# Rewriting the order of every engine as a table of slots: each step its own slot, three batches and 32 weight tiles placed one by one, then a repeating pattern; four feed-forward banks; most low halves of the weights taken by VectorE

## What is computed

```python
x = x + xattn(_layernorm(x), ctx, ctx, q_norm_w, k_norm_w, w_out)   # 16 heads, 4 key/value heads, causal
x = x + ffn(_layernorm(x), ...)
# xattn: q, k = rope(rms_norm(.) * w); attn = softmax(q k^T / sqrt(32) + causal mask); out = (attn v) @ w_out.T
# ffn, once for all batches: w = (w_q - 7.5) * scale per 64 columns, transposed     (4-bit codes, 512 x 2048 and 2048 x 512)
y1 = x1 @ w_up + b_up + x1 @ lora_a @ lora_b
x2 = relu(y1)
y2 = x2 @ w_down + b_down + x2 @ lora_a' @ lora_b'
```

## Time and profile before

| | |
|---|---|
| median of 3 runs | 587.93 us (584.47 to 588.89) |
| the profiled execution's own time | 587.63 us |
| its span, first to last instruction | 585.8 us |
| mean granted clock of TensorE | 0.929 of full speed (2.4 GHz) |
| first UP of batch 0 starts | 130.69 us into the span |
| result of batch 0 and of batch 15 written by DVE from | 171.8 us and 582.6 us |
| PE busy from the one to the other | 388.80 of 410.80 us |

### The profile page before, as it was taken

The page is one execution under the profiler, slowest core; times in us unless marked ns, Lnnn a source line. Parts: engine busy times, 40 slices in busy tenths (PEclk is TensorE's granted clock), DMA queues, the critical chain, the costliest instruction groups (busy, mean ns, idle before and its releaser), DMA issues.

```text
span 585.8 us, 12700 instructions
## 1 busy us (share of the span) xinstructions
PE 490.9 (84%) x4744; PEld 343.0 (59%) x4744; DVE 342.3 (58%) x1042; ACT 315.9 (54%) x947; POOL 301.4 (51%) x320
## 2 busy tenths in 40 slices
PE   0267456679888999989999989899999898999997
PEld 0134122337547676667677676767585757586783
DVE  2873513344456777675767758576767676564531
ACT  1557636373565665747484837383847464654210
POOL 3492474483174838383847556556657473625100
PEclk9999555759999999998999999899999998999999
DMA  8930652081053527180817282735455444536010
GB/s 171 284 84 2 191 131 62 29 190 32 10 89 88 123 56 139 39 167 10 167 21 157 39 138 47 131 61 118 56 122 98 84 95 57 103 52 109 2 38 18
DMA packets 144253, 52.87 MB, mean 90 GB/s; under 512 B 132768, under 2 KB 135088, under 8 KB 144144
## 3 DMA queue, kind: packets, MB, share of 16 engines
q1 hardware_dynamic: 141344, 51.56, 43.3%
q10 hardware_dynamic: 2768, 0.34, 0.5%
q0 software_dynamic: 80, 0.16, 0.1%
HBM read 16.39 MB, written 4.19 MB: 35 GB/s over the span
## 4 chain that ended last, share of the span: by engine, by line
PE 45%; POOL 20%; DMA 10%; issue 8%; ACT 6%; DVE 6%; SPq 5%; POOLq 0%; ACTq 0%; DVEq 0%
PE ff L767 19%; PE ff L782 8%; DMA pT<-big 8%; PE tb L748 8%; POOL big L396 6%; POOL pr L387 5%; PE ff L638 3%; SPq L326 3%; POOL y L436 3%; PE tb L735 2%; ACT pr L543 2%; PE sb L720 1%; PE ff L683 1%; POOL inv L379 1%; DVE x L978 1%
## 5 line engine op out<-in xcount | busy, mean ns | idle before, releaser
L767 PE MATMUL ff<-xnT,wu_hi 128*128 128x128 f16 x2048 | 184.2, 223 | 2.7 <-DVE y L1045 1.2
L767 PE MATMUL ff<-xnT,wu_lo 128*128 128x128 f16 x1024 | 180.4, 223 | 0.0
L767 PEld LDWEIGHTS ff<-xnT,wu_hi 128*128 128x128 f16 x2048 | 162.3, 100 | 13.7 <-issue 7.4
L782 PE MATMUL ff<-wd_hi,x 128*128 128x512 f16 x512 | 152.4, 379 | 3.1 <-DVE z L930 2.3
L387 POOL TENSOR_TENSOR pr<-pr,rinv 128x512 f32<-128x512 f32 x64 | 74.5, 1164 | 137.3 <-DVE rinv L911 137.3
L605 ACT ACTIVATE x<-z 128x512 f16<-128x512 f32 x64 | 40.3, 630 | 119.5 <-DVE z L930 119.5
L767 PEld LDWEIGHTS ff<-xnT,wu_lo 128*128 128x128 f16 x1024 | 102.4, 100 | 0.0
L543 ACT ACTIVATE pr<-pr,nmax 128x128 f32<-128x128 f32 x256 | 98.7, 388 | 4.3 <-DVE nmax L999 4.3
L782 PE MATMUL ff<-wd_lo,x 128*128 128x512 f16 x256 | 97.0, 379 | 0.0
L782 PEld LDWEIGHTS ff<-wd_hi,x 128*128 128x128 f16 x512 | 48.8, 98 | 63.4 <-issue 4.9
L396 POOL TENSOR_TENSOR big<-pr,big 128x512 f16<-128x512 f32 x64 | 78.7, 1238 | 3.4 <-ACT big L574 3.4
(11 more groups left out here) (139 smaller groups left out, 716.0 us busy)
## 6 DMA issues: line engine op xcount, KB each, us to landing
xt<-in_x SPq DMA_DIRECT2D x16, 256.0 KB, 3.1
big<-in_L_ffn_w_up_q SPq DMA_DIRECT2D x4, 1024.0 KB, 11.8
big<-in_L_ffn_w_down_q SPq DMA_DIRECT2D x4, 1024.0 KB, 5.4
out<-y SPq DMA_DIRECT2D x16, 256.0 KB, 2.5
kvt<-in_ctx SPq DMA_DIRECT2D x16, 64.0 KB, 3.3
wd_lo<-in_L_xattn_w_out SPq DMA_DIRECT2D x1, 1024.0 KB, 14.1
pT<-big SPq DMA_TRANSPOSE x64, 3.4
wd_hi<-in_L_ffn_w_up_lora_b SPq DMA_DIRECT2D x3, 128.0 KB, 8.6
```

Of the source, the lines that this page charges most:

```text
L767: last = pe.matmul(bank[:, P * h:P * h + P], a[:, m, cols], b[:, m, :], start=(h == 0 and m == 0 and i == 0), stop=(m == KC - 1 and i == 2 ...
L782: last = pe.matmul(ff[down_bank[n]][:], a[:, h, :], b[:, h, :], start=(h == 0 and i == 0), stop=(h == HC - 1 and i == 2))
```

## The change

The tables are replaced. Each operation of each engine now has its own table (`R_PHIGH`, `R_PLOW` and `R_PTURN` where `R_PSPLIT` served three engines), with four numbers: slots of batches 0, 1, 2 and 3; batch n from 3 on comes 264 slots after batch n-1. Each of the 32 tiles has a slot of its own for dequantising, turning, high half, rest and low half, and so have the five late loads, the lora pieces and the steps of w_out. Beside the order:

- the feed-forward has four banks (`ff0` to `ff3`); the bank of v's sum (`vb`) is given up, the sum goes into `tb[0]`, which PROJ also uses, and each waits for the other's reader;
- 22 of the 32 low halves are taken by DVE straight from bank minus high half (`weights_low`), without PE's subtraction; ten stay as they were;
- 17 tiles are dequantised by DVE (16 before), 15 by POOL; w_out is reordered by DVE instead of ACT; the scales of w_up are loaded from ACT's queue;
- the first tile waits for one lora copy (`a_copied`) instead of three.

The lora product opens a tile's bank and four turns add to it, as before.

```diff
-PERIOD = 8
-R_STATS, R_CENTRE, R_SINES, R_COSINES, R_ROPE = (0, 1), (1, 2), (1, 3), (1, 4), (2, 6)
-R_KSPLIT, R_KLOW = (1, 3), (1, 4)
-R_QSPLIT, R_QLOW = (2, 7), (2, 8)
...
+PERIOD, FREE = 264, 3
+R_STATS = (0, 369, 517, 922)
...
+R_PROBS = ((343, 737, 1108, 1389), (373, 745, 1135, 1417), (431, 785, 1216, 1541), (454, 787, 1255, 1592))
...
+R_POW2 = (606, 1090, 1504, 1785)
+R_YBASE = (714, 1169, 1638, 2002)
...
-TILE_AT = tuple(2 + (3 * t) // 4 if t < UP_TILES else 14 + (t - 16) // 2 if t < 26 else t - 7 for t in range(TILES))
-DEQ_LEAD = 4
-DVE_TILES = tuple(range(0, TILES, 2))
-WOUT_AT = 4
+DVE_TILES = (1, 2, 4, 6, 8, 10, 12, 14, 16, 18, 20, 22, 24, 26, 29, 30, 31)
+LOW_BY_DVE = (1, 3, 4, 6, 7, 10, 13, 15, 16, 17, 18, 19, 20, 22, 23, 24, 25, 26, 28, 29, 30, 31)
...
+TURN_AT = (206, 224, 233, 295, 443, 451, 458, 468, 487, 488, 508, 534, 583, 593, 595, 601, 649, 666, 744, 764, 806, 810, 892,
+           896, 907, 923, 951, 974, 980, 995, 1058, 1073)
...
+LOAD_AT = (141, 513, 580, 682, 741)
...
+WO_ORDER_AT = (259, 307, 353, 367)
...
-    SLOTS = PERIOD * (B - 2) + R_RESULT[1] + 1
-
-    def at(s, r, after=0):
-        if s - after == r[0]:
-            return 0
-        n, rest = divmod(s - after - r[1], PERIOD)
-        return n + 1 if rest == 0 and 0 <= n < B - 1 else None
+    SLOTS = PERIOD * (B - FREE - 1) + R_STORE[FREE] + 1
+
+    def at(s, r):
+        if s in r[0:FREE]:
+            return r.index(s)
+        n, rest = divmod(s - r[FREE], PERIOD)
+        return n + FREE if rest == 0 and 0 <= n < B - FREE else None
...
-        ff = [bank("ff0"), bank("ff1")]
+
+        ff = [bank("ff0"), bank("ff1"), bank("ff2"), bank("ff3")]
         sbk = [bank("sb0"), bank("sb1")]
 
         tb = [bank("tb0"), bank("tb1")]
-        vb = bank("vb")
 
...
+        def low_of(t):
+            return (w_low_v, LOW_BY_DVE.index(t) + 1) if t in LOW_BY_DVE else (w_low, t + 1 - len([u for u in LOW_BY_DVE if u < t]))
+
+        def wait_lows(eng, last):
+            by_dve = len([u for u in LOW_BY_DVE if u <= last])
+            if by_dve <= last:
+                eng.wait_ge(w_low, last + 1 - by_dve)
+            if by_dve:
+                eng.wait_ge(w_low_v, by_dve)
...
+        def next_bank():
+            b = (last_bank + 1) % 4
+            return (b + 1) % 4 if b == down_holds else b
...
+            for t in range(TILES):
+                if TURN_AT[t] == s:
+                    last_bank = t % 4 if t < UP_TILES else 2 + t % 2
+                    tile_bank[t], tile_free[t] = last_bank, freed_by[last_bank]
+                    freed_by[last_bank] = low_of(t)
...
-                n = at(s, R_KLOW)
+                n = at(s, R_KTURN)
...
-                    if TILE_AT[4 * (g - W_RING) + 3] == s:
+                    if LOAD_AT[g - W_RING] == s:
...
-                for t in tiles_to_dequantise(s):
-                    if t not in DVE_TILES:
+                for t in range(TILES):
+                    if DEQ_AT[t] == s and t not in DVE_TILES:
                         dequant(t)
-                n = at(s, R_STATS)
-                if n is not None:
+                n = at(s, R_KEYS)
+                if n:
                     keys(n)
+                n = at(s, R_POW)
+                if n is not None:
+                    norm_factors(n)
...
-            def order_wout():
-                act.wait_ge(wout_in, 16)
-                for j in range(KC):
-                    act.activation(wo_nat[:, j, :].rearrange("p (n g d) -> p n g d", g=NG, d=HD),
-                                   wo_raw[:, j, :].rearrange("p (g n d) -> p n g d", g=NG, d=HD),
-                                   ACT.Copy).then_inc(wo_ordered, 1)
-
...
+                for t in range(TILES):
+                    if HIGH_AT[t] == s:
+                        weights(t)
+                    if LOW_AT[t] == s and t not in LOW_BY_DVE:
+                        weights_low(t)
...
-                if t < 2:
-                    pe.wait_ge(a_copied, 3)
-                else:
+                if tile_free[t]:
                     pe.wait_ge(*tile_free[t])
                 g, j = divmod(t, 4)
-                if t in (0, UP_TILES // 4):
-                    pe.wait_ge(b_high, 1 if t == 0 else 3)
-                    pe.wait_ge(b_low, 1 if t == 0 else 3)
                 bank = ff[tile_bank[t]]
+                if t in (0, 4, UP_TILES):
+                    pe.wait_ge(a_copied, 3 if t == UP_TILES else 1)
+                    pe.wait_ge(b_high, 1 if t == 0 else 2 if t == 4 else 3)
+                    pe.wait_ge(b_low, 1 if t == 0 else 2 if t == 4 else 3)
                 if t < UP_TILES:
                     a, b = a_up3[:, P * j:P * j + P], b_up3[:, 512 * g:512 * g + 512]
...
-                    if n > 0:
+                    if n == 0:
+                        pe.wait_ge(wo_low, NN)
+                    else:
                         pe.wait_ge(v_arg_ready, n)
-                    pe.matmul(vb[:, 0:1], ones[:], ssq[:, n % 2:n % 2 + 1], start=True, stop=True).then_inc(v_summed, 1)
+                        if projs_before[n] > 0:
+                            pe.wait_ge(x1_ready, projs_before[n])
+                    pe.matmul(tb[0][:, 0:1], ones[:], ssq[:, n % 2:n % 2 + 1], start=True, stop=True).then_inc(v_summed, 1)
...
-                ts = tiles_at(s)
-                for i, t in enumerate(ts):
-                    weights(t)
-                    if i > 0:
-                        weights_rest(t - 1)
-                if WOUT_AT <= s < WOUT_AT + NN:
-                    wout_turn(s - WOUT_AT)
+                for i in range(3):
+                    if LORA_TURN_AT[i] == s:
+                        lora_turn(i)
+                for t in range(TILES):
+                    if REST_AT[t] == s and t not in LOW_BY_DVE:
+                        weights_rest(t)
+                    if TURN_AT[t] == s:
+                        weights(t)
+                for m in range(NN):
+                    if WO_TURN_AT[m] == s:
+                        wout_turn(m)
                 feed_forward(s)
-                for t in ts[-1:]:
-                    weights_rest(t)
                 products(s)
...
+            def wout_order(j):
+                if j == 0:
+                    dve.wait_ge(wout_in, 16)
+                dve.tensor_copy(wo_nat[:, j, :].rearrange("p (n g d) -> p n g d", g=NG, d=HD),
+                                wo_raw[:, j, :].rearrange("p (g n d) -> p n g d", g=NG, d=HD)).then_inc(wo_ordered, 1)
+
+            def weights_low(t):
+                dve.wait_ge(w_high, t + 1)
+                hi, lo = ((w[:, t % 4, 512 * (t // 4):512 * (t // 4) + 512] for w in (wu_hi, wu_lo)) if t < UP_TILES else
+                          (w[:, t - UP_TILES, :] for w in (wd_hi, wd_lo)))
+                dve.tensor_tensor(lo, ff[tile_bank[t]][:], hi, ALU.subtract).then_inc(w_low_v, 1)

```

More of the change, by code:

```diff
@@ L38 @@
-R_UP, R_DOWN = (18, 27), (22, 31)
-R_RESULT = (26, 35)
+PERIOD, FREE = 264, 3
+R_STATS = (0, 369, 517, 922)
+R_SQUARES = (2, 373, 523, 935)
+R_MOMENTS = (0, 441, 529, 968)
+R_KEYS = (0, 326, 621, 979)
+R_POW = (23, 496, 666, 994)
+R_CENTRE = (3, 464, 655, 1033)
+R_SINES = (2, 458, 720, 1019)
+R_COSINES = (28, 487, 676, 1083)
+R_ROPE = (218, 525, 754, 1063)
+R_KSPLIT = (7, 559, 747, 1040)
+R_KLOW = (176, 563, 837, 1076)
+R_KTURN = (19, 675, 897, 1074)
+R_QSPLIT = (172, 543, 779, 1097)
+R_QLOW = (231, 542, 835, 1120)
@@ new lines, in build @@
+        freed_by, last_bank, down_holds = [None] * 4, 3, None
+        def next_bank():
+            b = (last_bank + 1) % 4
+            return (b + 1) % 4 if b == down_holds else b
+        projs_before, sums_before = {}, {}
+        for s in range(SLOTS):
+            n = at(s, R_VSUM)
+            if n is not None:
+                projs_before[n] = len(sums_before)
+            n = at(s, R_PROJ)
+            if n is not None:
+                sums_before[n] = len(projs_before)
+        for s in range(SLOTS):
+            for t in range(TILES):
[3 more added lines that the diff above has]
+                    freed_by[last_bank] = low_of(t)
@@ L256, in build @@
+                n = at(s, R_DOWN[g])
+                if n is not None and g == 0:
+                    last_bank = down_holds = 0 if n == 0 else next_bank()
+                    down_bank[n], down_free[n] = last_bank, freed_by[last_bank]
+                    freed_by[last_bank] = (down_read, n + 1)
+                if n is not None and g == 3:
+                    down_holds = None
         block = es.enter_context(nc.Block())
@@ L1031, in values @@
             def values(s):
[L1032 removed]
+                n = at(s, R_VARG)
                 if n is not None:
```

315 lines of the change are left out of this document (168 added, 147 removed).

## The result

The changed kernel takes **531.89 us** (median of 4 runs, 529.08 to 532.98) against 587.44 us for the kernel before beside it (4 runs, 584.47 to 588.89): a ratio of 0.905, 95% interval 0.900 to 0.910. The forecast was 539.0 with a range of 520 to 562, faster by over 1%. The profiled execution took 531.35 us, its span is 529.6, its mean granted clock 0.99.

A forecast was written before the change was run, and what follows sets the result against it. PE was taken to bound the later batches and waiting the head. First result 133, then 400.8 to the last result, then 3.2 made a span of 537.0; adding 1.8 and 0.3 gave 539 us, range 520 to 562.

The forecast's parts named there:

- the head's 133 us: Start of the kernel up to the first result: forecast at 133 us against 171.8, 39 us won.
- qT was started at 33.49 before and should be at about 28: Attention of batch 0: qT starts at about 28 us, so scores come at 33 and PV near 60, against 91.39.
- The rest of the head: From PV of batch 0 near 60 us: first UP near 83, then 50 us to the first result at 133.
- Rival 3: Head at full clock without gaps: first result at 122, gap 3, no rest, 520 us in all; chance 0.15.
- 22 x 0.63 = 14 us of PE at most, but most of it lay beside waits: Weight tiles: 22 subtractions leave PE, 14 us at most, counted only in the stretch from PV to the first result.
- The load order: Head: group 3's weight load, moved ahead of batch 1, starts at 36 us, some 22 us earlier than 58.56.
- 388.8 + 4 + 8 = 400.8: Fifteen later batches: PE's work, other waits and the gap near batch 2; 400.8 against 410.8, 10 us won.
- the 4 us of pattern waits: Later batches: 4 us in all left for waits such as those for xnT, x2's low halves and DVE.
- the gap at batch 2: Between batches 1 and 2: one gap of PE before PROJ of batch 2, put at 8 us, bounds 0 and 20.
- Rival 2: Later batches: the new pattern has its own wait, 1.7 us in each of 12 periods, 559 us; chance 0.13.
- 7.1 instead of 12.0 us: Later batches: POOL's way from the power to the last low halves, shortened by moving y, keys and one probability.
- PE has more to do between PROJ and the next PV: Later batches: PE has 19.5 us of work there, PV could follow after 13.4, so 6 us of slack.

The follow-up runs named there:

- Kernels 1 to 3: The changed kernel with w_up's scales back on SP's queue (513.38 us), SP waiting for the small loads before group 0 (517.33), or scales last on ACT's queue (529.94).
- kernel 1: The changed kernel with the load of w_up's scales put back from ACT's queue to SP's: 513.38 us.
- kernel 5: The changed kernel with all low halves made by PE's subtraction and ACT's copy, none by DVE: 554.54 us.
- kernel 7: The kernel before with the weight group loads ahead of the DMA transposes in their slot instead of behind: 579.99 us.
- kernel 6: The kernel before with the same 22 low halves taken by DVE, in the tile's own slot: 577.64 us.
- kernel 8: The changed kernel with POOL's y and keys put back between the power and the last low halves: 534.30 us.
- kernel 10: The kernel before with PROJ and the steps that hang on it one slot earlier, one UP behind PV: 603.84 us.
- kernel 3: The changed kernel with w_up's scales issued last on ACT's queue and b_nat second: 529.94 us.

## Why the prediction was right, and where it was not

**The direction and the size** were right: 539 against 531.9. SP's long halt, most of the half clock behind 60 us and the waits for pT are gone. But the head's 133 us is right only by luck, as the sum of two errors of opposite sign: start 15.8 us too late, the rest 14.3 us shorter than put down.

**The start failed.** The step was "qT was started at 33.49 before and should be at about 28", with scores at 33 and the load of group 3 at 36 us. Measured: 42.63, 48.8 and 51.44, 14 to 16 us late. The list of the change names the scales' load from ACT's queue, and the prediction gave it no cost, though moving a DMA off SP moves all that SP issues behind it. Kernels 1 to 3 show the cause: SP's large loads in flight ahead of the last small ones. With that undone group 3 loads at 35.43 us, as forecast, and the first result comes at 117.4.

**The rest of the head was sized too long.** From an untouched start it takes about 16 us less than 133. PV to first UP took 17.7 us where the working had 23; first UP to first result 43.1 where it had 50. PROJ of batch 0 took 2.80 us, not the 4.9 of half clock. Rival 3 (head at full clock, no gaps, 520) was thus the truer picture of this part, and the late start hid it; together they gave the forecast's number. Of the clock: full from 76 us on, just before that PROJ (77.16), but for 90 to 97 us, where PE had been busy for 2.98 of the 6 us from 85 to 91, and where the first two UPs took 8.22 us against 5.4 at full clock. Before, it was half until PROJ had run, at 111 us. The Trainium skill (TensorE: Matmul & The Clock Gate, Part 1: The HAM clock gate) says that the array runs at 2.4 GHz while PE is kept busy. Taken at its word it would have taken some 10 us off the sum; the trace agrees from PROJ on but for those 7 us, and by kernel 1 that is the right side. One reading of the prediction was wrong: "no other engine is at 60% there either" doesn't hold between 22 and 60 us, where ACT is busy for 27.78 of 38.00 us.

**The low halves were mis-sized.** The duration was right, "L978 with 0.69 us" against:

```profile
L989 DVE TENSOR_TENSOR wd_lo<-ff,wd_hi 128x512 f16<-128x512 f32 x14 | 9.5, 686 | 4.1 <-ACT wd_hi L570 4.1
```

The step "22 x 0.63 = 14 us of PE at most, but most of it lay beside waits" was judged by the old order, in which PE waited anyway. In the new one PE is the bound between 60 and 134 us (busy for 68.53 of 74.00), and the rests, their waits for ACT and the clock they cost come to about 23 us (kernel 5). A saving beside waits counts once the waits are gone.

**The load order** was called the cause of the old head and put first. Alone it brings the first result forward by 5.5 us (kernel 7), DVE's low halves alone 10.5 (kernel 6), of the 37.3 that the head gained in spite of a start 14 us late. The rest comes with the order as a whole; the runs don't divide it further.

**The fifteen batches** were put at 388.8 + 4 + 8 = 400.8 and took 391.8. PE's work was 385.31, 3.5 less, at clock 1.00 instead of 0.99; the 4 us of pattern waits were 0; the gap at batch 2 was sized at 8, and all idle time of the stretch is 6.5, of which 5.3 stand between 155 and 169 us. Rival 2 didn't occur.

**Why the wait for pT went** was half of what the prediction said. It had two terms. One was POOL's shorter way from the power to the low halves, "7.1 instead of 12.0 us". Measured are 9.4, and it isn't needed: kernel 8 has 12.4 and no wait that repeats. The other was that PE has more to do between PROJ and the next PV, 19.5 us, since PROJ stands one UP behind PV and not two. Measured are 19.4 in the changed kernel and in kernel 8, and that is the room in which 12.4 us of POOL fit. But PROJ's place gives this room only together with the order of the other engines: moved in the old order (kernel 10) it lengthened POOL's way to 16.3 us, since the second half of the normalised rows now stood ahead of the masks on DVE and waited for ACT. Which steps of the new order on DVE and ACT prevent that stays open.

## What to carry to other kernels

Read a head by its first 30 us: here a small load that everything hangs on had to be issued ahead of the first large one on *any* queue, and moving a DMA between queues has to be costed by what then starts earlier. Here one line back gives a version that beats both kernels: 513.38 us. Work that lies beside waits is free only as long as the waits stay, so when a change removes waits, cost the removed work as if it were on the path. And an order by hand holds together: one step moved earlier in an order whose other steps stand still cost 2.6 to 3.8% here, though each move looked like a shorter loop. And set a clock row beside the lengths of equal matmuls before building on it: here its first nines were half clock.

## What was not expected of the hardware

- With 1 MB of weight codes issued at 3.29 us and 2 MB more at 9.05, a small DMA on ACT's queue (one row of 128 floats for each of 16 partitions) took 14.80 us to issue, against 3.34 to 4.41 with the weights behind it. ACT could compute nothing meanwhile.
- The last small load of ACT's queue was usable at 28 to 31 us in four profiles with the weights ahead (`s_up` in kernel 3, `b_nat` in the changed kernel, 5 and 8), against 11.6 to 11.9 when issued ahead of them. In the changed kernel the chain gives `b_nat` 17.73 us and then 6.03 us to no releaser; the view of the DMA issues has it landed 23.7 us after its issue, which is the sum.
- PE with many short idle pieces between tiles is granted 0.76 of full speed while busy for 16.09 of 20.00 us (kernel 5, 130 to 150 us), and 1.00 while busy for 18.79 of 20.00 (changed kernel, 110 to 130 us).
- The same DVE instruction has other lengths in another order. The low half of relu's output (L939 before, L1025 after), with both tensor operands in SBUF, had a mean of 809 ns before and 1062 after, 16.2 us more in all, which is more than the 22 low halves added. What it ran beside wasn't examined. It cost the later batches nothing, since PE had no wait there.
